# Per-token attention over heads: two fp16 parts of a scaled q instead of three bf16 parts

## The reference

```python
kx = modulated_linear(x, s, k_...)            # [B, N, 512], weights scaled per batch, + k_b
q = k = v = kx.reshape(B, N, 16, 32)          # 16 heads of 32
scores = einsum('bnhd,bnjd->bnhj', q, k) / sqrt(32)   # per token: heads against heads
out = einsum('bnhj,bnjd->bnhd', softmax(scores), v)
x = x + modulated_linear(out, s, o_...)       # + o_b
x = x + L1(x, ids, ...)                       # layer norms with looked-up gains, a 3072 -> 512 -> 512 MLP, a layer norm
```

## Time and profile before

| what | value |
|---|---|
| median of 3 runs | 1047.45 us (1045.44 to 1047.92) |
| the profiled execution | 1047.42 us |
| its span, first to last instruction | 1045.6 us |
| mean granted TensorE clock | 0.966 of 2.4 GHz |
| busy: PE, DVE, POOL, ACT | 961.5, 748.3, 539.0, 398.2 us |

### The profile page before, as it was taken

One profiled execution on the slowest core, in us unless ns is written; L12 is line 12 of the kernel. 1 busy time (PEld: TensorE's weight loads), 2 busy tenths in 40 slices (PEclk: granted clock), 3 DMA queues, 4 the chain that ended last, 5 costly groups with the idle time before them and its releaser, 6 DMA issues. The chain is left out here.

```text
span 1045.6 us, 22815 instructions
## 1 busy us (share of the span) xinstructions
PE 961.5 (92%) x9132; PEld 850.5 (81%) x9132; DVE 748.3 (72%) x1185; ACT 398.2 (38%) x691; POOL 539.0 (52%) x544
## 2 busy tenths in 40 slices
PE   7688688999898999999898999999898999999987
PEld 6544478898787899898787898998887898989876
DVE  2677776878678686878677686869677786868542
ACT  3262334343244434344243344343343343443311
POOL 3334376656445555656545465646555474645351
PEclk9988799999899999999999999999999999999999
DMA  8721223332524233333424332333424233323110
GB/s 337 316 85 26 59 64 71 91 70 75 123 57 120 61 90 70 97 68 79 119 61 113 81 85 56 98 68 89 104 61 115 59 90 79 85 54 91 38 41 21
DMA packets 132697, 93.21 MB, mean 89 GB/s; under 512 B 107888, under 2 KB 110192, under 8 KB 130928
## 3 DMA queue, kind: packets, MB, share of 16 engines
q1 hardware_dynamic: 123088, 67.68, 26.0%
q0 software_dynamic: 4608, 16.78, 5.3%
q10 hardware_dynamic: 4896, 7.29, 2.5%
HBM read 58.93 MB, written 8.39 MB: 64 GB/s over the span
## 5 line engine op out<-in xcount | busy, mean ns | idle before, releaser
L1436 POOL TENSOR_TENSOR op1l<-ytmp,op1h 128x512 fp32r<-128x512 f32 x64 | 83.8, 1310 | 117.3 <-ACT op1h L786 116.8
L1375 POOL TENSOR_TENSOR small<-small,cst 128x1 f32<-128x1 f32 x96 | 22.0, 230 | 135.8 <-DVE small L1181 72.1
L360 PEld LDWEIGHTS att<-q,BD 128*128 128x128 bf16 x2048 | 74.9, 118 | 11.6 <-DVE BD L999 10.1
L360 PE MATMUL att<-q,BD 128*128 128x64 bf16 (+1 forms) x2048 | 75.1, 200 | 9.9 <-DVE BD L999 9.9
L360 PE MATMUL acc<-op0h,W1xh 128*128 128x256 f32 x256 | 74.9, 293 | 3.4 <-DVE op0l L1203 3.4
L360 PE MATMUL acc<-op1h,W1hh 128*128 128x256 f32 x256 | 78.0, 305 | 0.0
L360 PE MATMUL acc<-op1h,W1th 128*128 128x256 f32 x256 | 75.1, 293 | 0.0
L360 PE MATMUL acc<-op0h,W1sh 128*128 128x256 f32 x256 | 73.7, 288 | 0.0
L360 PE MATMUL acc<-op0l,W1xh 128*128 128x256 f32 x256 | 73.2, 286 | 0.0
L360 PE MATMUL acc<-op0h,W1xl 128*128 128x256 f32 x256 | 73.1, 286 | 0.0
L360 PE MATMUL acc<-op1l,W1hh 128*128 128x256 f32 x256 | 72.6, 284 | 0.0
(11 more groups left out here) (237 smaller groups left out, 3165.5 us busy)
## 6 DMA issues: line engine op xcount, KB each, us to landing
xb<-in_x SPq DMA_DIRECT2D x32, 256.0 KB, 2.8
out<-xb SPq DMA_DIRECT2D x32, 256.0 KB, 2.3
xraw<-in_xT SPq DMA_DIRECT2D x31, 256.0 KB, 3.0
BD<-q SPq DMA_DIRECT2D x124, 64.0 KB
BD<-v SPq DMA_DIRECT2D x124, 64.0 KB, 2.1
BD<-q SPq DMA_DIRECT2D x124, 32.0 KB
BD<-v SPq DMA_DIRECT2D x124, 32.0 KB, 1.9
ring<-in_k_wT ACTq DMA_DIRECT2D x12, 256.0 KB, 4.3
```

The source lines that it names most:

```text
L360: return e.matmul(o, a, b, start=start, stop=True, skip_group_check=True)
L1375: e.tensor_tensor(rs[:, 0:1], mv[:, 1:2], eps5, ALU.add).then_inc(done, 1)
L1436: e.tensor_tensor(op[slot]["l"][:, :, half(g)], four(ytmp[YT[n, g][0]]), op[slot]["h"][:, :, half(g)].bitcast(F32), ALU.subtract).then_inc ...
```

## The change

The bound of a token is the root of |x|^2 + |k_b|^2 + 1e-12, in units of 2^12. `squares(g)` (ACT) squares the token-major x, with the row's sum as an accumulator; `bounds(g)` (POOL) adds the constant and raises the sum to -1/2 and 1/2. q is divided by the bound while it is taken out of PSUM, so that it fits fp16: `q_hi(g)` (ACT) writes the first part, `q_lo(g)` (DVE) the second, both token-major into `qt`. One transposition of 32-bit words (`q_T`) puts both parts into `q12`. There is no third part: `q3`, `v3` and `BD3` are gone. The scores come out too small by the bound's square; `true_scale(g)` (POOL) multiplies them, between `less_max` and `exponential`, by the sum, which `w_T(g)` (DVE, a 128 x 32 transposition) has laid along the partitions. The values come out too small by the bound; `x_one(g)` multiplies the output projection by it. The bias o_b is therefore added to x by itself (`add_ob(g)`, POOL), and its matmul is gone.

```diff
 @block.sync
+            def load_sq(g):
+                if g:
+                    e.wait_ge(s["sqx"], g)
+                e.dma_start(xsq[:, :], A["x"][g * 128:g * 128 + 128, :]).then_inc(s["lsq"], 16)
             def blocks_q(g):
                 e.wait_ge(s["AV"], 2 * g)
-                e.wait_ge(s["qb"], 2 * g + 2)
+                e.wait_ge(s["qT"], g + 1)
                 for i in range(4):
-                    e.dma_start(BD12[quad(i), :, quad(i), :, :], q12[quad(i), :, :, :, :]).then_inc(s["bq"], 16)
-                e.wait_ge(s["qr"], 2 * g + 2)
-                for i in range(4):
-                    e.dma_start(BD3[quad(i), :, quad(i), :], q3[quad(i), :, :, :]).then_inc(s["bq"], 16)
+                    e.dma_start(BD[quad(i), :, quad(i), :, :], q12[quad(i), :, :, :, :]).then_inc(s["bq"], 16)
...
 @block.tensor, scores and values, for each j of 16
                     mm(both, diag(j, 0), q, start=(j % 8 == 0))
-                    mm(both[:, :, 0], diag(j, 0), third(q3, j))
-                    mm(both, diag(j, 1), q)
-                    i = mm(both[:, :, 0], diag(j, 2), q[:, :, 0])
+                    i = mm(both[:, :, 0], diag(j, 1), q[:, :, 0])
...
-                    mm(both, diag(j, 0), r12, start=(j % 8 == 0))
-                    mm(both, diag(j, 1), r12)
-                    i = mm(one, diag(j, 2), e12[:, c, 0])
+                    mm(both, diag(j, 0), e12[:, c, :].rearrange("p m t -> p (m t)"), start=(j % 8 == 0))
+                    i = mm(both.rearrange("p (m t) -> p m t", t=2)[:, :, 0], diag(j, 1), e12[:, c, 0])
...
 out_proj
-                mm(tok[0][:, :], selT[:, 1, :], tab[:, :]).then_inc(s["O"], 1)
+                i.then_inc(s["O"], 1)
...
 @block.scalar
+            def squares(g):
+                e.wait_ge(s["lsq"], 16 * (g + 1))
+                e.activation(xsq[:, :], xsq[:, :], ACT.Square, scale=2.0 ** -12, accum_out=tok_s[:, g % 4, 2:3]).then_inc(s["sqx"], 1)
-            def q_first(g): ...   (and q_second)
+            def q_hi(g):
+                e.wait_ge(s["A"], g + 1)
+                e.wait_ge(s["sc"], 2 * g + 2)
+                if g:
+                    e.wait_ge(s["qT"], g)
+                e.activation(qt[:, :, 0], tok[1 if g else 0][:, :], ACT.Copy, scale=inverse(g)).then_inc(s["qh"], 1)
             def exponential(g):
-                e.wait_ge(s["sub"], 2 * g + 2)
+                e.wait_ge(s["wS"], g + 1)
...
 @block.vector
+            def q_lo(g):
+                e.wait_ge(s["qh"], g + 1)
+                e.scalar_tensor_tensor(out=qt[:, :, 1], in0=tok[1 if g else 0][:, :], scalar=inverse(g), in1=qt[:, :, 0], op0=ALU.mult, op1=ALU.subtract).then_inc(s["ql"], 1)
             def q_T(g):
-                e.wait_ge(s["A"], g + 1)
+                e.wait_ge(s["ql"], g + 1)
                 if g:
-                    e.wait_ge(s["qr"], 2 * g)
+                    e.wait_ge(s["S"], 2 * g)
+                    e.wait_ge(s["VT"], g)
...
             def v_T(g): one transposition (of q12) instead of two
+            def w_T(g):
+                e.wait_ge(s["sc"], 2 * g + 1)
+                if g > 1:
+                    e.wait_ge(s["wS"], g - 1)
+                e.transpose(wT[g % 2][:, :], w32[g % 2][:, :]).then_inc(s["wt"], 1)
             def x_one(g):
                 e.wait_ge(s["O"], g + 1)
-                e.wait_ge(s[f"ld{g % 4}"], 16 * (g // 4 + 1))
-                e.tensor_tensor(xs[:, :], tok[0][:, :], xs[:, :], ALU.add).then_inc(s["x1"], 1)
+                e.wait_ge(s["xob"], g + 1)
+                e.scalar_tensor_tensor(out=xs[:, :], in0=tok[0][:, :], scalar=bound(g), in1=xs[:, :], op0=ALU.mult, op1=ALU.add).then_inc(s["x1"], 1)
...
 @block.gpsimd
-            def q_rest(g): ...   (and q_third)
+            def bounds(g):
+                y = tok_s[:, g % 4, :]
+                e.wait_ge(s["sqx"], g + 1)
+                ...
+                e.tensor_tensor(w32[g % 2][:, :], y[:, 2:3].to_broadcast([128, 32]), sum_b[:, :].to_broadcast([128, 32]), ALU.add).then_inc(s["sc"], 1)
+                e.wait_ge(s["sc"], 2 * g + 1)
+                ...
+                e.tensor_tensor(y[:, 0:2], w32[g % 2][:, 0:2], cst[:, 20:22], ALU.pow).then_inc(s["sc"], 1)
+            def true_scale(g):
+                e.wait_ge(s["sub"], 2 * g + 2)
+                e.wait_ge(s["wt"], g + 1)
+                c = SE[:, :].rearrange("p (t h) -> p t h", h=16)
+                e.tensor_tensor(c, c, wT[g % 2][:, :].unsqueeze(2).to_broadcast([128, 32, 16]), ALU.mult).then_inc(s["wS"], 1)
+            def add_ob(g):
+                ...
+                e.tensor_tensor(xs[:, :], xs[:, :], ob[:, :], ALU.add).then_inc(s["xob"], 1)
```

More of the change, by code:

```diff
@@ L106, in build @@
         cst = at("cst", [128, 24])
-        selT = at("selT", [128, 3, 128], BF16)
+        tok_s = at("tok_s", [128, 4, 4])
+        w32 = [at(f"w32{i}", [128, 32]) for i in range(2)]
+        wT = [at(f"wT{i}", [128, 32]) for i in range(2)]
+        sum_b = at("sum_b", [128, 1])
+        selT = at("selT", [128, 2, 128], BF16)
         tab = at("tab", [128, 512], BF16)
@@ L1258, in _ @@
                 table_rows(n)
+            q_lo(0)
             q_T(0)
+            w_T(0)
             hidden_add()
@@ L1272, in _ @@
             a_sum(0)
+            q_T(1)
+            w_T(1)
             vectors()
@@ L1344, in _ @@
                     if more:
+                        q_lo(a + 2)
                         q_T(a + 2)
+                    w_T(b)
                     score_sum(b)
                     less_max(b)
+                    e_T(b)
                     v_stats(a)
-                    e_T(b)
                     e_second(b)
```

229 lines of the change are left out of this document (114 added, 115 removed).

## The result

The changed kernel takes 1054.26 us (median of 4 runs, 1051.23 to 1054.83), beside 1047.68 us for the kernel before in the same rounds (4 runs, 1045.44 to 1049.58). The ratio is 1.0058, 95% interval 1.003 to 1.0085: slower by 0.6%, some 6 us. The forecast was 1064, a growth of 17 us; so it had the direction and overstated the size. The profiled execution took 1051.23 us with a span of 1049.2, 3.6 us more than before. It is the fastest of the four; the other three took 1054.3 to 1054.8 us at a mean granted clock of 0.960 to 0.962, where it had 0.963. So what follows accounts for 3.6 us of the growth, and the rest, some 3 us, is in no trace.

The account below looks back on a forecast made before the run. The prediction took TensorE, and equally tightly the softmax behind the scores, to bound the kernel. Terms of +11, +4, +2 and +1 gave +18 on the 1045.6 us span, 1063.6, and with 1.8 around it 1065, stated as 1064; range 1036 to 1078.

Parts of the forecast that it names:

- seven pairs without weights, with the clock: Pairs without weights to modulate: +0.5 us each, plus 1.1 for the clock's fall; +11 us over seven.
- six pairs with weights: Pairs with weights to modulate: VectorE's queue +1.5 us at `e_second(a)`; +0.7 per pair, +4 us; bounds -0.8 and +2.
- ahead of the loop and pairs 0 and 1: Ahead of the loop: fewer block copies (-1.2 us), but `true_scale` queued behind weight splits; together +2, bounds -4 and +6.
- last pair: The last pair of tiles: +1 us.
- The second bound: Softmax between the first matmuls of `scores` (S) and `values` (V): 0.3 and 0.2 us to spare, as tight as TensorE.
- TensorE's gain: Matmuls removed from `scores`, `values` and selT: 1.83 us per tile, 58.6 us over 32 tiles if TensorE bounded everything.
- The gap ahead of V(a): TensorE idle 2.9 us before tile a's first `values` matmul, at 14.15 us after the first `scores` matmul instead of 12.3.
- The clock behind that gap: Behind tile a's 2.9 us gap the clock falls to half, costing about 1.5 us; at odds of 0.75, +1.1 per pair.
- the clock stays: Rival: the clock is held through the new gaps; -8, giving 1056 us; chance 0.25.
- The rival of the short gap: Rival, tile a: port free, gap under 2.2 us, no clock fall; 1040 us (1034 to 1045); chance 0.15.
- Tile b: First `values` matmul 12.5 to 12.8 us after first `scores` matmul, TensorE idle 0.5 to 0.8; `W2` about 4.2 later.

Follow-up runs that it names:

- e1: The kernel before without the matmuls of the third bf16 parts and the output-bias matmul, casts and copies kept: 1038.98 us, ratio 0.987.
- e3: The kernel after without the multiply `true_scale`, so its scores lack the bound: 1025.76 us, ratio 0.976 to the kernel before.
- e7: The kernel after with a second GpSimd multiply, by ones, behind `true_scale`: 1095.95 us, ratio 1.044 to the kernel before.
- e6: The kernel after with the multiply by the bound on VectorE, behind the subtraction, instead of GpSimd: 1074.67 us, ratio 1.023 to the kernel before.
- e2: The kernel before with one call moved, `v_stats(a)` behind `e_T(b)`: 1049.03 us, ratio 0.9985.
- e18: The kernel after with five changes of order at once, and the loads of x's second copy moved on SyncE: 1013.65 us, ratio 0.967 to the kernel before.
- e10: The kernel after with `q_lo(a+2)` and `q_T(a+2)` moved behind tile b's subtraction on VectorE: 1033.77 us, ratio 0.985 to the kernel before.
- e14: The kernel after with `affine(pb)` ahead of tile a's multiply and `add_be(pb)` behind it: 1050.50 us, ratio 1.000 to the kernel before.
- e4: The kernel after with squares and bounds of tile a+2 moved later, behind parts of the gated products: 1049.11 us, ratio 0.998 to the kernel before.
- e17: The kernel after with squares and bounds of a+2 and b+2 late, and later loads of x's second copy: 1042.46 us, ratio 0.995 to the kernel before.

## Why the prediction came out as it did

The forecast had the sign, and each of the four terms of its sum failed in size:

| term | forecast, us | measured, us |
|---|---|---|
| seven pairs without weights, with the clock | +11 | 0.0 |
| six pairs with weights | +4 | +15.5 |
| ahead of the loop and pairs 0 and 1 | +2 | -6.5 |
| last pair | +1 | -5.4 |
| sum | +18 | +3.6 |

That it came out slower at all, as forecast, is in part luck: the loss that was forecast, in pairs without weights, wasn't there, and another one was.

**The second bound: right.** That matmuls alone are not worth 3.7 us a pair, because the softmax behind S has 0.2 to 0.3 us to spare, is what e1 shows (1.2 us).

**TensorE's gain: about right.** 1.83 us per tile was forecast. `scores` fell by 1.1 us and `values` by 0.5; over the page it is 49 us instead of 58.6. Of the 9 us between, 8 are in the six pairs with weights, where TensorE ran longer at half clock.

**The gap ahead of V(a): mis-sized, and the step that failed first.** Forecast 2.9 us with V(a) at 14.15; measured 1.61 with V(a) at 13.49. The multiply with its hand-over was taken at 1.4 us; the exponential starts 0.8 later than before (7.9 behind S, not 8.5): the multiply takes 1.06, not 1.3, and the subtraction ends at 6.7 instead of 7.1, since `affine` no longer runs beside it, which I had counted for tile b and not for tile a. `q_lo(b)`, 0.8 us on VectorE ahead of the sum, was counted at nothing in tile a; it ends with the exponential and cost nothing more, but it is why e3 wins so little in tile a. The sum of the exponentials starts 0.6 later than before, and the collision of `affine` with the division adds 0.8, as described, with the same 0.55 us: 1.4 together, where 2.1 was forecast. TensorE arrived at 11.9, not at 11.2: it had waited 0.33 us for `op0l` (Gt's matmuls); the other 0.3 were not traced.

**The clock behind that gap: the term that failed with it.** "Seven pairs at +0.5 + 1.1 give +11": measured 0.0. The pair came out at +0.1 instead of +0.5, and no fall followed a gap of 1.6 us. The odds and the price were sound for a gap of 2.7 to 2.8, as e7 and e6 show (six of seven each, 1.2 to 1.5 us), though of the five gaps that the odds came from one, at 113.2 us, stood where the clock was at half already; the term hung wholly on the length of the gap, and 1.3 us less of it took all 8 us away. The rival "the clock stays" had the clock right but held the pair at +0.5. The rival of the short gap (under 2.2, no fall) had the gap right, but for a free port, and the port was not free.

**Tile b:** V(b) - S(b) was forecast at 12.5 to 12.8, measured 12.1, without a wait. V(b) to W2 was forecast at 4.2 and measured 4.88: the squares were seen, the collision of `add_ob` with `silu_lo` was not. The two errors cancel.

**The pairs with weights: the other term that failed, mis-sized.** +0.7 each was forecast with +2 as the bound; measured +2.6. I had followed VectorE's queue from `e_second(a)`, and taken it as 1.5 us late, which is what it is (1.4 in pair 7). But the chain that ends last leaves that queue: `finish`, a store, the load of x behind it on SyncE, the split, and then squares and bounds ahead of the product whose buffer the weights need. The late x is +0.9 in pair 7 (+1.4 in the mean of pairs 3, 7 and 11) and squares and bounds are +1.0. Every part was in the code, and the trace before names x as what ScalarE waited for. And the clock, which falls in these pairs already, was taken as unchanged; it stayed at half for 34.1 us instead of 23.9. The errors of the two terms, -11 and +11.5, cancel almost wholly.

**The ends:** +2 ahead of the loop and +1 for the last pair were forecast; measured -6.5 and -5.4. e2 shows 4.1 of the last pair's: `v_stats(a)` no longer holds tile b. Ahead of S(0) TensorE comes 0.5 us later and waits 6.8 us for a block copy instead of 9.9, which is the 2.6; the 3.9 in pairs 0 and 1 were not tested. As the errors above cancel, these two terms are where a sum of +18 became +3.6: forecast +3, measured -12.

**What stays open:** how much of the lateness in pairs 4, 8 and 12 is the second copy's traffic and how much is the request that comes later. The copy has a part, since moving it took 3.0 us of waits for raw weights away in e18; one execution of each kernel, with pairs that differ by the clock alone, doesn't size it. Why the clock stays at half for 6.8 us behind some gaps and for 3.4 or not at all behind others of the same length, no run shows.

## What to carry to other kernels

When an instruction is put into a chain that has no slack, look first at what each in-order queue does while it waits: moving two VectorE operations into the wait beside the multiply gave 2% (e10 against the kernel after), more than the 1.3% of all the saved matmuls alone (e1). A transfer that is issued behind a store inherits the lateness of the work before that store, so a chain of waits has to be followed through the DMA queue as well, in the stages that differ and not in the plain one alone. Before two kernels are compared pair by pair, the granted clock of the pairs has to be read beside them: it made 2.7 us between two pairs of one kernel that waited alike. And a term that is there wholly or not at all (here the fall of the clock behind a gap) should be forecast with the length of the gap as a range, not at one value.

## What the hardware showed beyond the expected

- GpSimd's multiply of 128x512 fp32 with a broadcast second operand took 1.06 us, where its instructions of the same size with two full operands took 1.27 to 1.29 (medians, kernel after).
- The same multiply on VectorE took 1.67 us beside GpSimd's `affine`; VectorE's subtraction took 0.69 alone and 1.11 to 1.17 beside it (e3, e6, e14).
- A square with an accumulated sum is followed by a separate read of the accumulator of 0.18 to 0.19 us.
- The two powers of `bounds` (128x2) took 0.71 us, one (128x1) 0.55.
- The same load of 256 KB landed 6.6 us after its issue in the pair with weights shown (7.2 before the change) and 8.4 us in e4, where the page's median is 3.1.
- Behind gaps of 2.7 to 2.8 us, in the pairs without weights of e6 and e7, the clock was granted at half (1.2 GHz) 12 times of 14; behind gaps of 1.6 us in the kernel after never in seven, nor behind gaps ahead of values(b) of 2.02 us in e17 and 2.07 in e1.
